# Two-bank alternation for the last node blocks and an earlier end of the edge counts in a graph network's first layer

## The reference

```
h_out = clifford_linear(h + h_agg, upd_w, upd_b)
x     = layernorm(x + h_out)
```

## Time and profile before

| what | value |
|---|---|
| runs (3) | 3445.0 us median, 3444.54 to 3446.77 |
| profiled execution | 3448.08 us |
| its span, first to last instruction | 3446.2 us |
| TensorE / VectorE / ScalarE / GpSimd busy | 84% / 70% / 73% / 70% |
| mean granted TensorE clock | 0.915 |
| layer 0's quads and blocks, about | 210 to 1651 us of the span |

### The profile page before, as it was taken

How to read it: one execution, slowest core, us unless ns; L and a number is a source line. 1 busy time by engine, 2 the same in 40 slices (tenths; PEclk the granted TensorE clock), 3 DMA queues, 4 the chain that set the end, 5 groups by cost and what they waited for, 6 DMA issues and landing times. The chain is left out here.

```text
span 3446.2 us, 53363 instructions
## 1 busy us (share of the span) xinstructions
PE 2889.8 (84%) x16283; PEld 2462.8 (71%) x16283; DVE 2428.2 (70%) x5413; ACT 2502.4 (73%) x3761; POOL 2418.0 (70%) x2267
## 2 busy tenths in 40 slices
PE   4769888888888888888599999868999967889996
PEld 3558777877777777776477777647777755777775
DVE  6968777788887788877466666546666655677776
ACT  1067666667766777665499999569999937999992
POOL 2367777777777777774577777577777757777774
PEclk6579999999999999998699999979999988999998
DMA  4256555555555555554656666475666547566663
GB/s 130 70 148 164 149 156 156 158 158 148 158 159 152 156 159 148 158 153 116 200 184 185 190 185 191 124 232 181 186 189 193 184 128 220 185 192 198 201 197 103
DMA packets 327863, 572.44 MB, mean 166 GB/s; under 512 B 47877, under 2 KB 225878, under 8 KB 327574
## 3 DMA queue, kind: packets, MB, share of 16 engines
q0 software_dynamic: 105696, 290.56, 30.3%
q1 hardware_dynamic: 218361, 275.92, 25.8%
q10 hardware_dynamic: 3517, 2.48, 0.3%
HBM read 494.21 MB, written 74.56 MB: 165 GB/s over the span
## 5 line engine op out<-in xcount | busy, mean ns | idle before, releaser
L1452 POOL DMA_INDIRECT rows_arena<-table_h,src_idx x1224 | 1323.2, 1081 | 482.5 <-issue 368.7
L1452 POOL DMA_INDIRECT rows_arena<-table_scaled_x,src_idx x782 | 847.3, 1083 | 378.5 <-issue 279.8
L2014 PE MATMUL bank<-wide_counts,h_pairs 128*128 128x512 f32 x3528 | 893.6, 402 | 30.3 <-ACT wide_counts L1599 29.4
L1599 ACT CAST wide_counts<-rows_arena 128x1024 fp32r<-128x1024 bf16 (+1 forms) x450 | 905.8, 2013 | 0.0
L2014 PEld LDWEIGHTS bank<-wide_counts,h_pairs 128*128 128x128 f32 x3528 | 654.3, 192 | 194.0 <-issue 50.8
L1951 PE MATMUL bank<-rel_pairs,ftype_hot 125*128 125x258 f32 x4688 | 748.0, 310 | 50.9 <-ACT ftype_hot L1578 50.9
L1951 PEld LDWEIGHTS bank<-rel_pairs,ftype_hot 125*128 125x128 f32 x4688 | 658.8, 202 | 82.6 <-ACT ftype_hot L1578 51.0
L1788 DVE TENSOR_TENSOR row_pairs<-rows_arena,row_pairs 128x1024 fp32r<-128x1024 f32 x306 | 374.3, 1223 | 407.6 <-ACT row_pairs L1587 404.8
L1974 PE MATMUL bank<-row_pairs,rel_pairs 128*128 128x256 f32 x2448 | 387.2, 303 | 209.1 <-DVE row_pairs L1788 208.6
L1974 PEld LDWEIGHTS bank<-row_pairs,rel_pairs 128*128 128x128 f32 x2448 | 332.0, 200 | 244.2 <-issue 241.0
L1587 ACT CAST row_pairs<-rows_arena 128x1024 fp32r<-128x1024 f32 x306 | 321.4, 1050 | 201.7 <-DMA rows_arena<-table_h,src_idx 168.2
(11 more groups left out here) (185 smaller groups left out, 3064.2 us busy)
## 6 DMA issues: line engine op xcount, KB each, us to landing
rows_arena<-edge_counts SPq DMA_DIRECT2D x234, 512.0 KB, 3.9
edge_counts<-fcount SPq DMA_DIRECT2D x48, 832.0 KB, 6.7
rows_arena<-in_edge_type_dram SPq DMA_DIRECT2D x195, 187.5 KB
rows_arena<-table_h,src_idx POOLq DMA_INDIRECT x1224, 3.6
rows_arena<-table_h SPq DMA_DIRECT2D x36, 512.0 KB, 11.7
rows_arena<-table_scaled_x,src_idx POOLq DMA_INDIRECT x782
table_h<-chunk_info SPq DMA_DIRECT2D x96, 128.0 KB, 4.2
rows_arena<-in_x_dram SPq DMA_DIRECT2D x6, 1024.0 KB
```

What stands on the lines that cost most here:

```text
L1452: pool.indirect_dma_start(out=rows[:, g % ring, c, :], out_offset=None, in_=table[:, :], in_offset=bass.IndirectOffsetOnAxis(ap=src_idx[:, ...
L1599: act.copy(wide_counts[:, v % HALVES, 0:n, :].rearrange("p b c -> p c b"), count_tile[:, t % ATILES, :, b % HTILE:b % HTILE + n]).then_inc ...
L2014: last = pe.matmul(bank[2 + h][:, 0:PASS_COLS], h_pairs[:, v % HALVES, part, b % HALF, h * P:(h + 1) * P], wide_counts[:, v % HALVES, b % ...
```

## The change

Two things change in layer 0. The counts fall on 190 of the 196 steps: `counts_at` divides by `2 * (NG - 6)`, so the last position is 378 instead of 390. And blocks that start behind the quads (`start[j] >= NG`; these are 47 and 48) alternate between bank 6 and bank 0, and a block behind such a block starts two steps later instead of three. Block 48 so starts at step 200 in bank 0, and its product no longer waits for `s_y` (`bank_given(48)` is 0, since no node block used bank 0 before); the loop has 207 steps.

```diff
+COUNTS_EARLY = 6
@@ starts
-                start.append(max([ready[b]] + ([start[j - 1] + (3 if first else 1)] if j else []) +
+                apart = 1 if not first else 2 if j and start[j - 1] >= NG else 3
+                start.append(max([ready[b]] + ([start[j - 1] + apart] if j else []) +
                                  ([start[j - WORK] + 10] if j >= WORK and norm else [])))
@@ counts_at
-                return [i for i in range(ND if first else 0) if i * 2 * NG // ND == position]
+                return [i for i in range(ND if first else 0) if i * 2 * (NG - COUNTS_EARLY) // ND == position]
@@ banks
-                vec_bank = bank[6][:, D:2 * D]
+                behind_quads = [j for j in range(NB) if first and start[j] >= NG]
+                def node_bank(j):
+                    return bank[0] if j in behind_quads and behind_quads.index(j) % 2 == 1 else bank[6]
+                def vec_bank(j):
+                    return node_bank(j)[:, D:2 * D]
+                def bank_given(j):
+                    return max([i + 1 for i in range(j) if node_bank(i) is node_bank(j)], default=0)
...
-                    return bank[6] if first else bank[(0, 7)[j % 2]]
+                    return node_bank(j) if first else bank[(0, 7)[j % 2]]
@@ product
-                            if first and j >= 1:
-                                pe.wait_ge(s_y, j)
+                            if first and bank_given(j):
+                                pe.wait_ge(s_y, bank_given(j))
```

More of the change, by code:

```diff
@@ L1645, in _ @@
                                         act.wait_ge(s_o, b - 1)
-                                    act.copy(vT[:, b % 2, :], vec_bank).then_inc(s_vT_cp, 1)
+                                    act.copy(vT[:, b % 2, :], vec_bank(b)).then_inc(s_vT_cp, 1)
                                 if s + 2 < NG:
@@ L1858, in give @@
                             y = node_tile(b)
-                            step(dve.tensor_tensor(y, vec_bank, y, ALU.add))
+                            step(dve.tensor_tensor(y, vec_bank(b), y, ALU.add))
                             dve.sem_inc(s_y, 1)
@@ L2069, in turn @@
                             for h in range(DH):
-                                last = pe.transpose(vec_bank[:, h * P:(h + 1) * P],
+                                last = pe.transpose(vec_bank(b)[:, h * P:(h + 1) * P],
                                                     vec[:, b % 2, h * P:(h + 1) * P], ident[:])
@@ L2076, in update @@
                             for h in range(DH):
-                                last = pe.matmul(vec_bank, vT[:, b % 2, h * P:(h + 1) * P],
+                                last = pe.matmul(vec_bank(b), vT[:, b % 2, h * P:(h + 1) * P],
                                                  wT["upd"][:, h, :], start=(h == 0), stop=(h == DH - 1))
```

## The result

| | before | after |
|---|---|---|
| median of 15 runs each, us | 3444.54 (3433.77 to 3450.19) | 3453.52 (3445.09 to 3464.36) |
| ratio to before | | 1.0033, 95% interval 1.0024 to 1.0042 |
| profiled execution: time / span, us | 3448.08 / 3446.2 | 3451.04 / 3449.2 |
| end of layer 0's last normalisation, us from the span's start | 1651.0 | 1661.9 |

The changed kernel is slower, by 8 to 14 us (0.2 to 0.4%). The two profiled executions differ by only 3.0 us in span, since layers 1 to 3, which the change does not touch, took 7.9 us less in the one of after (1787.3 us; in the later traces of e1 to e4, e13 and e16 they took 1790 to 1798).

What follows compares the result with a forecast made beforehand. TensorE was taken to bound layer 0's body, with repeated waits for ScalarE's count copies; a chain of waits bounds the end. From 3445.0, -13.5 + 3.3 + 3.6 + 4 - 0.9 + 0.7 = -2.8 gave 3442.2 us, range 3434 to 3451.

Steps and rivals of the forecast that it cites:

- rival B: Stalled steps, at ScalarE's root in step start + 4: denser counts lengthen the stalls further, total +8.5 us, 3453.5; chance 0.17.
- the dear kind: Stalled steps with the last ring clearing 5 or 6 half steps ahead: 18.35 us on average, against 15.60 for the nearest.
- Step 1: Steps 190 to 195 lose their counts and holes: 43.62 us become 29.17, taken as -13.5 us.
- D: Last steps, 190 to 195: GpSimd's gathers set the pace, 38.5 us instead of about 30, total +5.6, 3450.6; chance 0.05.
- Step 2: Eleven counts move ahead of step 190: nine in unstalled steps cost +3.3 us, stalled step 163 regains one for +3.6.
- Steps 2 and 3: Stalled steps before 190: +3.6 us for step 163's regained count, +4 for ring clearings falling elsewhere.
- the table: Stalled steps' average times sorted by half steps since VectorE's last count-ring clearing: applied to the new schedule, +7.0 us.
- Step 4: Block 46: without the last count's addition between, VectorE's take starts earlier and all behind it follows, -0.9 us.
- Step 5: Blocks 47 and 48 behind the quads: product 48's removed wait is replaced by others, the end gets +0.7 us longer.
- C: End behind the quads: the second bank removes a 3.3 us stretch, total 6.8 us below, 3438.2; chance 0.08.
- A: Stalled steps keep their sum, neither clearings nor step 163 cost anything: total -10.4 us, 3434.6; chance 0.25.

Runs made afterwards that it cites:

- e1: Kernel before with only the change's counts schedule (last position 378), banks and starts as before: ratio 1.0034, 3457.4 against 3445.6 us.
- e2: Changed kernel with the counts as before, so only the banks and block 48's nearer start differ from before: ratio 0.9998.
- e3: Kernel before with ScalarE's root of a block at the end of its step and the normalisation one step later: 3350.3 us, ratio 0.9728.
- e4: Changed kernel with ScalarE's root of a block at the end of its step and the normalisation one step later: 3343.5 us, ratio 0.9710.
- e13: Kernel before with the last 32 counts packed on half steps 358 to 379, earlier counts unmoved, on a usual chip: ratio 1.0024.
- e16: Kernel before with its 18 half steps without a count each put at a stalled step's first position, on a usual chip: ratio 0.9934, 23 us faster.
- e14: Kernel before without the 44 ring clearings (counts come out wrong), on a usual chip: stalled steps with the ones behind them 691.8 us.
- e15: Changed kernel without the ring clearings (counts come out wrong), on a usual chip: stalled steps with the ones behind them 703.8 us.
- the late fill: On slow chips, kernel before with the last 32 counts packed on half steps 358 to 379, earlier counts unmoved: ratios 0.9985 and 0.9979.

## Why the prediction was wrong

The forecast was -2.8 us with a range up to 3451; measured were +9.0 in the medians and +10.9 in layer 0. All terms but those of the stalled steps were forecast at -10.4 together and measured at -12.9. So the stalled steps alone, +7.6 forecast and +23.8 measured, turned the sign. The sign and the size are those of rival B (+8.5), and so is its mechanism in general: the dense counts lengthen the stalls. B's own working was another: it had three more steps change to the dear kind, and the kinds have just the members that the prediction counted.

- *Step 1, steps 190 to 195: right.* 29.17 were worked out, 29.22 measured; the 0.9 us allowed for block 45 did not come. D is refuted: full clock, no wait for a gather.
- *Step 2, counts in unstalled steps: right*, +3.3 forecast, +4.1 measured. Step 163 went, with the step behind it, from 14.36 to 19.47, +5.1 where I had +3.6.
- *Steps 2 and 3, the stalled steps: the step that failed.* The sum had +3.6 for step 163 and +4 for the 43 others, half of a table that said +7.0. Measured were +5.1 and +18.7 (e1 against e2: +4.7 and +22.3). There were two errors.
  - *I halved the table as perhaps chance.* It was not. Take each step's mean of the two traces with either schedule (before and e2, after and e1). The seven steps that the table made dearer by 2.4 to 3.0 us rose by 3.7 on average; the seven that it made cheaper by 1.5 to 3.4 fell by 2.3. What the distance stands for is more than the clearing's own time, though: between e14 and e15, which have no clearings, the same two groups still moved by +1.0 and -1.9.
  - *I gave free half steps a price only at a stalled step's first position*, which is one of the 17. The other ten that were lost had no term. Some 12 to 15 us of the 43 steps are beyond the whole table. They may well be there: the 21 steps that have one free half step fewer in the five steps ahead of them rose by 0.9 each, the 19 that have as many as before by 0.1. But between e14 and e15 the two groups do not differ (0.2 and 0.2). So this cause is argued and not shown, and it stays open. e16 gives the worth of a free half step at the best place alone, 2.4.
- The granted clock says why the price is above the work: over steps 2 to 189 it falls from 0.95 to 0.93, with 12.2 us more of idleness and some 11.6 us more for the same products.
- *Step 4, block 46: too small.* From the last sums to take 47 it took 11.7 us before and 9.2 after, 2.5 less. The earlier take is 0.9 of it, as forecast. Update 46 ran in 1.13 instead of 1.95 us, at the full clock level, with a gap of 0.65 us ahead of the turn where there had been 1.52; product 47 with its picks was 0.4 shorter, and the last 0.4 lie before the last window's addition.
- *Step 5, the last two blocks: right in each order.* Take 48 came 7.5 us behind take 47 instead of 8.0, earlier than I had it, and block 48's copy waited for block 47's root as told; from take 47 on, +0.2 instead of +0.7. C is refuted, by e2 for itself.
- *A* fell: the stalled steps did not keep their sum. Its argument, that single steps scatter, was weaker than it looked: the same schedule repeats in the 44 steps with their successors to 2 and 5 us of 750.

## What to carry to other kernels

Before squeezing the gaps out of a regular schedule, ask what the engines do with them: here a denser schedule cost 24 us in regularly stalled steps, and a price read in a step without stalls did not hold there. Before moving work away from a stall's end, look at what stands behind the stalled instruction: here one square root of 0.20 us, placed ahead of two copies of other data, cost 95 us, where the second bank was to remove a gap of 3. A second buffer did nothing while the next link was an engine's own order, and gave 1.0 us once that order was changed.

## What the runs showed of the hardware that was not expected

Chips differed. On three of those that were used (0, 12 and 15) the kernel before took 3864 to 3925 us, on chips 1 and 3 it took 3444 to 3446. The instructions last nearly as long there (in layer 0 the median gather of L1452 took 1.04 instead of 0.98 us), but 14 to 26 of the 100 steps without a stall take over 11 us. In the traces of these chips VectorE's messages (L1718) wait 98 to 131 us for something that the profile cannot name, of which before has none; what it is is not shown. Two of the comparisons came out otherwise there: e16's kernel was up to 0.4% slower instead of 0.7% faster, and the late fill was not measurably slower. A schedule tuned on such waits should be timed on more than one chip.
